# Two attention layers in fp32 pairs on one core: rings of 16 exponential tiles, and the orders of all four engines around attention rewritten

## The reference, cut to what matters

```
for (gamma, beta, wq, bq, wk, bk, wv, bv, wp, bp, eps) in two layers:   # x: (2, 32, 32, 256), N = 1024, C = 256
    xn = group_norm(x, 32 groups of 8 channels, eps) * gamma + beta
    q, k, v = xn @ wq + bq, xn @ wk + bk, xn @ wv + bv
    attn = softmax(q @ k.T / 16, axis=keys)
    x = (attn @ v) @ wp + bp + x
```

## Time and profile before

| | |
|---|---|
| median of three runs | 274.82 us |
| profiled execution | 275.11 us, its span 273.3 us (so 1.8 us lie around the span) |
| PE busy | 258.9 us, 95% of the span |
| DVE, ACT, POOL busy | 172.9, 151.5, 110.5 us |
| TensorE clock granted | at the full level in all 40 slices |
| POOL waiting for exponentials (`p_low`) | 107.9 us |

### The profile page before, as it was taken

How to read it: one execution, slowest core, us unless ns; L and a number is a source line. 1 busy time by engine, 2 the same in 40 slices (tenths; PEclk the granted TensorE clock), 3 DMA queues, 4 the chain that set the end, 5 groups by cost and what they waited for, 6 DMA issues and landing times.

```text
span 273.3 us, 4591 instructions
## 1 busy us (share of the span) xinstructions
PE 258.9 (95%) x1650; PEld 233.5 (85%) x1650; DVE 172.9 (63%) x436; ACT 151.5 (55%) x295; POOL 110.5 (40%) x111
## 2 busy tenths in 40 slices
PE   3999899999979999999989999999999999999994
PEld 2788688889978899879988899879988899889993
DVE  0499576786685557475976557475976547554623
ACT  3465454499867607670686616680577506670650
POOL 2016200186444814461264723471064733550680
PEclk9999999999999999999999999999999999999999
DMA  5960000000000000000000000000110000100102
GB/s 169 329 235 1 0 1 2 0 0 2 0 1 2 1 2 0 0 1 2 0 1 2 0 2 0 0 0 2 40 41 0 1 22 19 38 2 19 48 12 77
DMA packets 5965, 7.37 MB, mean 27 GB/s; under 512 B 556, under 2 KB 4664, under 8 KB 5944
## 3 DMA queue, kind: packets, MB, share of 16 engines
q1 hardware_dynamic: 5920, 7.08, 7.7%
q10 hardware_dynamic: 24, 0.01, 0.0%
HBM read 4.99 MB, written 2.10 MB: 26 GB/s over the span
## 4 chain that ended last, share of the span: by engine, by line
PE 61%; DVE 20%; ACT 9%; issue 6%; POOL 1%; DMA 1%; DVEq 0%; ACTq 0%; POOLq 0%
PE ring L910 9%; PE ring L912 9%; PE ring L911 9%; PE O L949 6%; PE O L951 6%; PE O L950 6%; DVE S L641 4%; DVE xn_lo L570 3%; ACT S L400 3%; DVE xnat L651 2%; ACT P_hi L399 2%; DVE xraw L563 2%; DVE t_lo L606 2%; ACT S L392 2%; PE ring L896 2%
## 5 line engine op out<-in xcount | busy, mean ns | idle before, releaser
L285 POOL TENSOR_TENSOR P_lo<-S,P_hi 128x512 fp32r<-128x512 f32 x64 | 82.9, 1302 | 107.9 <-ACT S L400 107.9
L949 PE MATMUL O<-V,P_hi 128*128 128x258 f32 x208 | 59.9, 288 | 0.0
L951 PE MATMUL O<-V,P_lo 128*128 128x258 f32 x208 | 58.9, 283 | 0.0
L950 PE MATMUL O<-V,P_hi 128*128 128x256 f32 x208 | 58.8, 282 | 0.0
L392 ACT COPY S<-ring 128x512 f32<-128x512 f32 x64 | 37.5, 587 | 37.6 <-PE ring L912 34.8
L910 PE MATMUL ring<-t_hi,xn_lo 128*128 128x512 f32 x128 | 51.4, 402 | 0.8 <-DVE t_lo L606 0.8
L399 ACT ACTIVATE P_hi<-S 128x512 fp32r<-128x512 f32 x64 | 40.6, 635 | 19.8 <-DVE S L641 18.1
L912 PE MATMUL ring<-t_hi,xn_hi 128*128 128x512 f32 x128 | 50.1, 392 | 0.0
L911 PE MATMUL ring<-t_lo,xn_hi 128*128 128x512 f32 x128 | 50.0, 391 | 0.0
L624 DVE TENSOR_TENSOR R<-ring,R 128x512 f32<-128x512 f32 x48 | 33.0, 688 | 24.7 <-ACT S L392 24.0
L641 DVE TENSOR_TENSOR S<-X,S 128x512 f32<-128x512 f32 x64 | 42.3, 681 | 0.0
(11 more groups left out here) (114 smaller groups left out, 407.5 us busy)
## 6 DMA issues: line engine op xcount, KB each, us to landing
xnat<-in_x SPq DMA_DIRECT2D x8, 256.0 KB, 6.8
out<-xnat SPq DMA_DIRECT2D x16, 128.0 KB, 1.9
wide<-in_vectors SPq DMA_DIRECT2D x2, 384.0 KB, 7.2
w_wq<-in_L_conv_wq SPq DMA_DIRECT2D x2, 256.0 KB, 4.9
w_wk<-in_L_conv_wk SPq DMA_DIRECT2D x2, 256.0 KB, 5.0
w_wv<-in_L_conv_wv SPq DMA_DIRECT2D x2, 256.0 KB, 6.7
w_wp<-in_L_conv_wp SPq DMA_DIRECT2D x1, 256.0 KB, 6.8
w_wp<-in_L_conv_wo SPq DMA_DIRECT2D x1, 256.0 KB, 6.9
```

The costliest lines, as they stand in the source:

```text
L285: nc.gpsimd.tensor_tensor(P_lo[:, tile, :], S[:, tile, :], P_hi[:, tile, :].bitcast(F32), ALU.subtract).then_inc(po_P, 1)
L949: nc.tensor.matmul(bank[:, 0:C + 2], P_hi[:, tile, mine], v[:, kb, 0:C + 2], start=(kb == 0), stop=False)
L950: nc.tensor.matmul(bank[:, 0:C], P_hi[:, tile, mine], v[:, kb, C + 2:VX], start=False, stop=False)
L951: last = nc.tensor.matmul(bank[:, 0:C + 2], P_lo[:, tile, mine], v[:, kb, 0:C + 2], start=False, stop=(kb == NB - 1))
```

## The change

- `P_hi` and `P_lo` become rings of 16 tiles, with an index of their own (`exp_of`); S stays at 12. The exponentials of chunk c now wait for the attention of chunk c - 2 as a whole.
- On PE, in `attention`, the maxima of the following chunk are transposed after key block 4 of query block 0, and its shifts after key block 1 of query block 1; they stood behind blocks 0 and 1. The group statistics' two small matmuls stand two score blocks sooner. The next unit's t stands behind query block 1 of the attention of `first`, and stood behind block 2. The last attention takes key blocks 0 to 3 by keys, and then, behind one wait for all its P_lo, key blocks 4 to 7 by queries.
- On DVE, the shifted tiles stand together in rows and ahead of outputs; `query_shift` stands ahead of the output beside it; the statistics, the affine map and `normalise` are spread between the running maxima of `second`.
- On ACT, the exponentials of `first` stand together ahead of the score copies of `second`; six instead of four exponentials of the last chunk of a unit stand in that unit; the t tiles stand between them.

Core of the diff:

```diff
+    P_TILES = 16
+    def exp_of(c, kb):
+        return (c * NB + kb) % P_TILES
...
             def exponentials(c, kb):
-                if c * NB + kb >= TILES:
-                    act.wait_ge(pe_O, ((c * NB + kb - TILES) // NB + 1) * QB)
+                if c > 1:
+                    act.wait_ge(pe_O, (c - 1) * QB)
...
-            for kb in range(1, 4):
+            for kb in range(1, 6):
+                if kb == 5:
+                    t_high(1, 0, 0)
                 exponentials(1, kb)
-            for k in range(KC):
-                t_high(1, 0, k)
+            t_high(1, 0, 1)
...
             query_shift(1)
+            for kb in range(2):
+                shifted(1, kb)
             for q in range(2):
                 xn_low(1, q)
-            for kb in range(2):
+            for kb in range(2, 4):
                 shifted(1, kb)
             for q in range(2, TQ):
                 xn_low(1, q)
-            for kb in range(2, 4):
+            for kb in range(4, NB):
                 shifted(1, kb)
             for j in range(QB):
                 output(0, j)
                 if j in (1, 3):
                     t_low(1, 0, j // 2)
-            for kb in range(4, 6):
-                shifted(1, kb)
...
                     for kb in range(NB):
                         attend(c, j, kb)
-                    if j == 0:
-                        maxima_by_query(following)
+                        if (j, kb) == (0, 4):
+                            maxima_by_query(following)
+                        if (j, kb) == (1, 1):
+                            shift_to_all(following)
                     if j == 1:
-                        shift_to_all(following)
                         before_third()
...
+                    if more and kb == 2:
+                        mean_of_groups(u + 1)
                     if more and kb == 4:
-                        mean_of_groups(u + 1)
-                    if more and kb == 6:
                         variance_of_groups(u + 1)
-                attention(first, second, lambda: None, next_first_half)
-            for kb in range(NB):
+                attention(first, second, next_first_half, lambda: None)
+            for kb in range(NB // 2):
                 attention_by_keys(CHUNKS - 1, kb)
+            pe.wait_ge(po_P, CHUNKS * NB)
+            for j in range(QB):
+                for kb in range(NB // 2, NB):
+                    attend(CHUNKS - 1, j, kb)
```

More of the change, by code:

```diff
@@ L434, in _ @@
                     if m in (2, 5):
-                        exponentials(before, 4 + m // 3)
+                        exponentials(before, 6 + m // 3)
                 for kb in range(NB):
                     score_copy(first, kb)
-                    if kb in (0, 2):
-                        exponentials(before, 6 + kb // 2)
                     if more and kb in (3, 6):
                         raw_rows(u + 1, kb // 3 - 1, Z)
[L444 to L451, removed]
+                for kb in range(NB):
+                    if kb in (3, 4):
+                        t_high(u, 1, kb - 3)
+                    if more and kb == 6:
+                        raw_rows(u + 1, 2, Z)
+                    exponentials(first, kb)
                 for kb in range(NB):
@@ L462, in _ @@
                         xn_high(u + 1, q)
-                for kb in range(3):
+                for kb in range(6):
+                    if more and kb in (2, 3):
+                        t_high(u + 1, 0, kb - 2)
                     exponentials(second, kb)
[L465 to L469, removed]
+            for kb in range(6, NB):
                 exponentials(CHUNKS - 1, kb)
@@ L697, in _ @@
                     v_low(u, m)
-                    if m in (2, 5):
+                    if u > 1 and m in (1, 4):
                         shifted(before, 6 + m // 3)
@@ L714, in _ @@
-                shifted(first, 3)
+                shifted(first, 6)
+                shifted(first, 7)
                 output(before, 2)
-                shifted(first, 4)
                 if more:
                     statistics_of(u + 1, 2)
-                shifted(first, 5)
                 output(before, 3)
[L721 to L733, removed]
+                if more:
+                    statistics_of(u + 1, 3)
+                    channel_statistics(u + 1)
@@ L734, in _ @@
+                running_max(second, 1)
+                running_max(second, 2)
+                if more:
+                    group_deviation(u + 1)
+                running_max(second, 3)
+                if more:
+                    variance(u + 1)
+                running_max(second, 4)
                 if more:
                     affine_map(u + 1)
+                running_max(second, 5)
+                if more:
+                    normalise(u + 1, range(1))
+                running_max(second, 6)
@@ L737, in _ @@
+                if more:
+                    normalise(u + 1, range(1, 2))
+                running_max(second, 7)
+                if more:
+                    normalise(u + 1, range(2, TQ))
+                query_shift(second)
                 output(first, 0)
-                query_shift(second)
                 if more:
-                    normalise(u + 1)
                     xn_low(u + 1, 0)
                     xn_low(u + 1, 1)
-                output(first, 1)
                 shifted(second, 0)
@@ L745, in _ @@
                 shifted(second, 1)
+                if not more:
+                    shifted(second, 2)
+                    shifted(second, 3)
+                output(first, 1)
                 if more:
@@ L748, in _ @@
                     xn_low(u + 1, 3)
-                output(first, 2)
-                shifted(second, 2)
-                if more:
+                    shifted(second, 2)
                     t_low(u + 1, 0, 0)
-                shifted(second, 3)
-                if more:
+                    shifted(second, 3)
                     t_low(u + 1, 0, 1)
[L756 to L760, removed]
+                    output(first, 2)
+                    shifted(second, 4)
+                    shifted(second, 5)
+                    output(first, 3)
+                else:
+                    for kb in range(4, NB):
+                        shifted(second, kb)
+                    output(first, 2)
+                    output(first, 3)
             for j in range(QB):
```

28 lines of the change are left out of this document (13 added, 15 removed).

## The result

The changed kernel takes 273.2 us (median of seven runs, 272.7 to 273.75) and the kernel before 275.27 (seven runs) beside it: a ratio of 0.9913, 95% interval 0.9897 to 0.9928. That is 2.1 us faster. Forecast was 4.5 us. The span of the profiled execution fell from 273.3 to 271.3 us.

A forecast was written before the change was run, and what follows sets the result against it. PE's own work was taken as the bound, so only its waits and the tail could be won: 1.56 + 1.4 + 0.8 + 0.9 - 0.2 = 4.5 us, giving 270.3 us as a median; range 269.3 to 272.5.

The forecast's parts named there:

- Unit statistics: Units 1 and 2: both PE waits for `var_c` go, as DVE computes it behind an earlier maximum; 1.56 us won.
- Border to unit 1: Start of unit 1: the wait for `t_lo` at about 79 us stays, the second wait goes; 0.8 us won.
- The end: Last attention by queries: only one output left behind PE's last matmul, P_lo ready in time by 1.3 us; 0.9 us won.
- Tight maxima and shifts: Inside attention: last maximum 0.1 us to spare, query shift 0.3 us; 0.2 us charged in all.
- Borders of units 2 and 3: Starts of units 2 and 3: PE's `w_row` waits of 0.90 us each shrink to 0.2 us; 1.4 us won.
- At the later borders 3 us of slack take this up: Later unit borders: 3 us of slack would absorb a delay from DVE and POOL blocking each other, which was placed at unit 1.
- about 2.2 us sooner: In attention: shifted tiles, exponentials and P_lo of a chunk start about 2.2 us sooner, worth nothing in itself.
- I reckon bank 3 free about when PE wants it: Value block 7 at units 2 and 3: `v_high` 3, behind exponential pair 6, is nearly on time; 0.2 us left of each wait.
- The rival that named the blocking: Unit 1: two `xn_low` quarters each wait a whole POOL P_lo (1.3 us), PE 2.6 us late; 272.9 us, chance 0.08.
- The rival that the waits only move: Unit borders: PE's wait passes to `v_low` 5 to 7 behind ACT's exponentials; 2.4 us won, 272.4 us, chance 0.11.
- The other two rivals: Late maxima and shifts at six places, 271.6 us, chance 0.15; affine map delaying maxima, slower, 276.9 us, chance 0.06.
- The sum's upper end: Whole kernel: if everything in reach went, the time would be 269.4 us.

## Why the prediction was wrong, point by point

The direction was right, the size was not: 2.1 us for 4.5, and 273.2 us lies above the range's end of 272.5. Part of the miss is the kernel before itself, which took 275.27 beside the changed one and 274.82 in the runs that the forecast stands on: the same gain from there gives 270.8. The other 2.4 us are one step.

- **Unit statistics, 1.56 us: right.** Both waits went. The map and `normalise` between the maxima made nothing late. That this part carries the others too (5.5 us when put back) was not seen.
- **Border to unit 1, 0.8 us: right.** 1.74 us of cost became 0.80, so 0.94. The wait for `t_lo` stayed, at 79.67 us, as was said.
- **The end, 0.9 us: right.** From 271.05 - 269.35 = 1.70 behind PE's last matmul to 269.05 - 268.26 = 0.79. P_lo was there with 1.4 us to spare at halfway (262.4), forecast 1.3; alone, the part loses the 2.0 less 0.9 that its working gives.
- **Tight maxima and shifts, -0.2 us: nothing lost.** The tenth of a microsecond held.
- **Borders of units 2 and 3, 1.4 us: wrong, and the step that failed.** They cost 1.84 us before and 2.77 after, a loss of 0.9: 2.3 us from the forecast, nearly all of the miss. Two sentences failed. "At the later borders 3 us of slack take this up" put the blocking of DVE by POOL where it did not happen, at unit 1 (both pairs of `xn_lo` took 1.28 us there; POOL waited instead, 1.70 us for a P_lo), and took it as harmless at the others. In units 2 and 3 it fell in full, 2.2 us, and the 3 us are DVE's ("DVE has work for about 3 us less there"), while exponential pairs 4 and 5 on ACT and the value copies behind them were not counted. The added POOL wait shows this by itself: the wait at block 4 went. P_lo also came nearer to DVE's work than was reckoned: "about 2.2 us sooner" was the shift alone, and the first P_lo of this chunk starts 7.4 us into the attention (130.19 - 122.77) where it started 11.0 in (135.01 - 124.00), 3.6 sooner. And "I reckon bank 3 free about when PE wants it", 0.2 us, was too small: 0.35 is left without the block, and 0.80 with it.
- **The rival that named the blocking** had the mechanism, the rows and the price of a P_lo; it had the wrong place, and a chance of 0.08. That its 272.9 us lies by the measured 273.2 is luck: it lost 2.6 us at unit 1, where nothing was lost, and what was lost came at units 2 and 3, by another path.
- **The rival that the waits only move** was half right: a wait behind ACT's exponentials did appear, at value block 7 (for `v_low` 3, not for 5 to 7 as it said), and moving exponential pairs 6 and 7 took it away. But the wait at block 4 did not pass over to it; it stayed, and the two together cost more than the one before. The other two rivals did not happen: PE has no new wait for R or `neg_shift`.
- **The sum's upper end.** "If everything in reach went" is 269.6 us by its own terms (0.4, 0.1 and 0.2 more than the forecast), not 269.4. Nothing hangs on it.

Of the 2.0 us between the spans, 1.56 + 0.94 + 0.91 - 0.93 = 2.5 are placed; the first score matmul started 0.7 us later in the profiled execution after (29.55 for 28.81), and 0.2 the other way is not placed.

## What to carry to other kernels

When a chain is started sooner, look for who else uses its engines and ports at the new time: the first P_lo moved 3.6 us ahead, onto two-input subtractions of DVE. With the exponentials put ahead of the value copies, this turned the 1.4 us that were to be won at two borders into 0.9 lost, half of the forecast gain. In-order queues turn such a block into a wait several engines further on, so a slack is counted at each queue behind the delayed step, not only at the nearest reader. Where two users block each other, holding back the one with time to spare is a gain: one wait on POOL was worth 2.5 us by the ratios, 2.1 by PE's own costs. And parts of a reordering can be worth less than nothing alone, as the end by queries was.

## What the runs showed of the hardware

A DVE subtraction with both inputs in SBUF and a POOL subtraction did not run at once at any place looked at: whichever came second stood for the rest of the other's run, but for the last 0.1 us or so. At unit 1 of the changed kernel it is POOL, whose P_lo takes 1.70 us for 1.30 while the `xn_lo` beside it keep their time:

```profile
69.56 1.28 DVE L567 TENSOR_TENSOR xn_lo<-xraw,xn_hi 128x512 fp32r<-128x512 f32 x2
...
70.31 1.70 POOL L289 TENSOR_TENSOR P_lo<-S,P_hi 128x512 fp32r<-128x512 f32 x1 [3.34 <-ACT S L404]
```

The kernel before had the same at unit 2, harmless, since DVE came first: its `xn_lo` ran from 134.20 to 135.49, and the first of two P_lo took 1.64 us:

```profile
135.01 2.89 POOL L285 TENSOR_TENSOR P_lo<-S,P_hi 128x512 fp32r<-128x512 f32 x2 [8.54 <-ACT S L400]
```

A shifted tile, which has one input in PSUM and one in SBUF, was not held: two of them took 1.28 us at 70.76 beside the P_lo of 70.31, as elsewhere.

In "SBUF — State Buffer" of the Trainium skill, section "Who interferes with whom", the order of issue decides who blocks; the trace agrees.

The clock was a surprise. In the kernel with rings of 12, PE stood idle for 2.9 us twice, and the granted clock fell from 1.00 to 0.50, that is from 2.4 to 1.2 GHz, for about three microseconds behind the first wait and six behind the second (0.62 on the mean from 183 to 186 us): a score matmul of 0.40 us took 0.63 there. Its steps went from 0.23 to 0.42 us (115.10 to 115.52, with the next at 115.95). The steps between 113.78 and 117.15 us add up to 1.6 us more than their usual lengths, and those between 179.24 and 185.24 to 2.9: 4.5 us in all, and the kernel lies 4.8 above its expectation of 276 us. (Some tenths of this are no matter of the clock, since the step behind a wait is 0.10 us longer at the full clock too.) In the kernel with the end by queries alone PE stood for 2.0 us, at 264.6 to 266.6, and the granted clock was 1.00 from 255 to 275 us.
